# Delta-rule layers: the triangle's inverse made in full from 32x32 products, and one solution step in 32x32 tiles

## The reference

```python
def delta_rule(q, k, v, beta):
    def step(W, inp):
        qt, kt, vt, bt = inp
        wk = jnp.einsum('bhde,bhe->bhd', W, kt)
        v_new = bt * (vt - wk)
        W = W + jnp.einsum('bhd,bhe->bhde', v_new, kt)
        out = jnp.einsum('bhde,bhe->bhd', W, qt)
        return (W, out)
    ...
def fast_ff(x, ln_g, ln_b, slow_w, out_w):
    h = layer_norm(x, ln_g, ln_b)
    qkvb = jnp.einsum('sbi,oi->sbo', h, slow_w).reshape(slen, bsz, H, 3 * D + 1)
    q, k, v, beta = jnp.split(qkvb, [D, 2 * D, 3 * D], axis=-1)
    q = jax.nn.softmax(q, axis=-1)
    k = jax.nn.softmax(k, axis=-1)
    beta = jax.nn.sigmoid(beta)
    attn = delta_rule(q, k, v, beta)
```

## Time and profile before

| | us |
|---|---|
| median of 3 runs | 5387.88 |
| lowest, highest | 5385.71, 5416.66 |
| the profiled execution | 5345.09 |
| its span, first to last instruction | 5343.3 |

### The profile page before, as it was taken

How to read it: one execution, slowest core, us unless ns; L and a number is a source line. 1 busy time by engine, 2 the same in 40 slices (tenths; PEclk the granted TensorE clock), 3 DMA queues, 4 the chain that set the end, 5 groups by cost and what they waited for, 6 DMA issues and landing times. The chain is left out here.

```text
span 5343.3 us, 141254 instructions
## 1 busy us (share of the span) xinstructions
PE 4536.1 (85%) x57740; PEld 2868.5 (54%) x57741; DVE 2973.0 (56%) x5849; ACT 2153.1 (40%) x4123; POOL 853.9 (16%) x2139
## 2 busy tenths in 40 slices
PE   3678888888988988998777987799999999985995
PEld 1247777773437777774354654345454455443663
DVE  3445444453024444454577887488685885864343
ACT  1123232332123333231365566177575775741221
POOL 0000000000000000000454555011111111102112
PEclk7779888898988888798888988899999999996997
DMA  1000000000000000000100000000000000005223
GB/s 42 2 7 3 3 3 3 3 3 18 0 6 3 3 3 3 3 3 3 38 1 1 1 1 1 10 1 0 1 0 1 1 0 1 0 3 194 87 85 100
DMA packets 47557, 85.79 MB, mean 16 GB/s; under 512 B 7120, under 2 KB 38128, under 8 KB 46064
## 3 DMA queue, kind: packets, MB, share of 16 engines
q1 hardware_dynamic: 40944, 61.84, 3.4%
q0 software_dynamic: 6144, 16.79, 1.0%
HBM read 45.05 MB, written 33.55 MB: 15 GB/s over the span
## 5 line engine op out<-in xcount | busy, mean ns | idle before, releaser
L1769 PE MATMUL psum<-hm_ex,hm_mix 128*128 128x512 f32 x1024 | 510.9, 622 | 42.1 <-ACT hm_Aq L1849 38.1
L1835 ACT ACTIVATE hm_ex<-psum,hm_nm 128x1024 f32<-128x1024 f32 x256 | 285.5, 1115 | 300.6 <-DVE hm_nm L1893 300.6
L1769 PEld LDWEIGHTS psum<-hm_ex,hm_mix 128*128 128x128 f32 x1024 | 175.7, 191 | 353.1 <-issue 345.4
L1908 DVE COPY hm_A<-psum 128x1024 f32<-128x1024 f32 x256 | 312.9, 1222 | 51.5 <-PE psum L1778 47.8
L1903 DVE TENSOR_SCALAR_CACHE_REDUCE hm_plus<-hm_Aq,hm_cbcol,hm_sums 128x1024 f32<-128x1024 f32 x256 | 340.5, 1330 | 0.0
L1893 DVE TENSOR_REDUCE hm_nm<-psum 128x1 f32<-128x1024 f32 x256 | 311.1, 1215 | 14.5 <-PE psum L1757 14.5
L1778 PEld LDWEIGHTS psum<-K,hm_Aq 128*128 128x128 f32 x2048 | 236.7, 140 | 149.9 <-issue 145.2
L957 DVE TENSOR_TENSOR fw_M<-fw_M,psum 128x256 f32<-128x256 f32 x256 | 107.9, 421 | 344.9 <-PE psum L728 342.4
L1307 ACT ACTIVATE pt_signs<-pt_acts,pt_tb 128x1024 f32<-128x1024 f32 (+1 forms) x224 | 227.8, 1020 | 146.7 <-POOL pt_tb L1180 104.4
L1840 ACT ACTIVATE hm_junk<-hm_Aq 128x1024 f32<-128x1024 f32 x256 | 270.6, 1057 | 30.3
L1757 PE MATMUL psum<-hm_kt,hm_qd 64*32 64x512 f32 x4096 | 280.9, 607 | 0.0
(11 more groups left out here) (380 smaller groups left out, 9117.4 us busy)
## 6 DMA issues: line engine op xcount, KB each, us to landing
ex_rows_in<-ex_zero SPq DMA_DIRECT2D x2, 5120.0 KB, 24.8
ex_xs<-ex_rows_in SPq DMA_DIRECT2D x80, 128.0 KB, 2.0
ex_rows_out<-ex_ys SPq DMA_DIRECT2D x80, 128.0 KB, 1.7
ex_w<-in_ex_w SPq DMA_DIRECT2D x2, 4096.0 KB, 23.0
X<-in_x SPq DMA_DIRECT2D x2, 2048.0 KB, 12.5
out_y<-X SPq DMA_DIRECT2D x2, 2048.0 KB, 9.0
ff_w<-in_ff_w SPq DMA_DIRECT2D x2, 1024.0 KB, 5.9
pt_w_proc<-in_pt_proc SPq DMA_DIRECT2D x1, 2048.0 KB, 7.6
```

The costliest lines, as they stand in the source:

```text
L1769: mm = pe.matmul(bank[4 + c], mix[:, u, :], ex[:, u, 512 * c:512 * c + 512], start=True, stop=True)
L1835: act.activation(ex[:, u, :], flat2(psum[:, 2 * u:2 * u + 2, :]), ACT.Exp, bias=nm[:, u:u + 1], accum_out=rsum[:, u:u + 1]).then_inc(s_ex, 1)
L1908: dve.tensor_copy(A[:, :, :, QT_ * t:QT_ * t + QT_], flat2(psum[:, 6:8, :]).rearrange("p (m g n) -> p m g n", m=MT, g=HEADS)).then_inc(s_a ...
```

## The change

The inverse of the whole 32-token triangle is made for each group and head: with N the product of Z and the off-diagonal rest, the inverse is Z + (I - N + NN)(-NZ). It takes five more calls of `product`: the turn of `z3` by a unit matrix (`zn`, copied by ScalarE), the product `z3` and `loff` in both orientations (`nn`, copied with a factor of -1), then in the next body `nn` squared and `zn` by `nn`, and last `s1` by `nz`. VectorE makes `s1` in `series` and the inverse in `inverse`. `solve` is called once, as 8 heads x 4 groups = 32 matmuls with 32x32 weights and 64 columns. The copies `r0`, the eight copies of `spread` into `z3x` and `ntx`, and the two calls of `solution` are gone; `solved` copies from PSUM instead of adding, and stands ahead of `softmax` on VectorE. `turn` moves ahead of the products with `loff` on TensorE, and the copies of `tr` with it on ScalarE. Banks 2 and 5 are shared by halves. The diff, cut to its core:

```diff
-                def product(left, right):
+                def product(b, at, left, right, sig):
                     for n in range(HEADS):
+                        for c in range(4):
+                            mm = pe.matmul(bank[b][rows(c), at + DH * n:at + DH * n + DH], right[rows(c), n, :],
+                                           left(rows(c), n), start=True, stop=True)
+                    mm.then_inc(sig, 1)
...
+                def solve(a):
+                    for n in range(HEADS):
+                        hd = DH * (2 * (n % 4) + n // 4)
                         for b in range(4):
...
+                            mm = pe.matmul(bank[2][rows(b), 64 * n:64 * n + 64], inv[rows(b), n, :],
+                                           rhs[rows(b), a % 2, :, hd:hd + DH], start=True, stop=True)
+                    mm.then_inc(s_ap, 1)
...
                     if so:
-                        pe.wait_ge(s_zx, s + 1)
-                        solve(z3x, given, s_y)
                     if ch:
                         pe.wait_ge(s_trc, i + 1)
                         pe.sem_inc(s_go, 1)
                         gram(a, 0, s_ga)
+                    if so:
+                        pe.wait_ge(s_nn, s + 1)
+                        pe.wait_ge(s_zn, s + 1)
+                        pe.sem_inc(s_go, 1)
+                        product(5, 0, of(nn[:, 0]), nn[:, 1], s_nb)
+                        product(2, C, of(zn), nn[:, 0], s_nb)
...
-                    if so:
-                        pe.wait_ge(s_nt, s + 1)
-                        pe.wait_ge(s_r0, s + 1)
-                        solve(ntx, first, s_ap)
                     if rc:
                         pe.wait_ge(s_m, r * 5 + 2)
                         through_state(ra, 1)
+                    if so:
+                        pe.wait_ge(s_s1, s + 1)
+                        pe.wait_ge(s_nz, s + 1)
+                        pe.sem_inc(s_go, 1)
+                        product(2, 0, of(s1), nz, s_nc)
...
                         project(i + 1)
-                    if so:
-                        pe.wait_ge(s_rk, s * 2 + 1)
-                        solve(ntx, later, s_ap)
...
                     if rc:
                         pe.wait_ge(s_m, r * 5 + 3)
                         through_state(ra, 2)
+                    if so:
+                        pe.wait_ge(s_ix, s + 1)
+                        pe.sem_inc(s_go, 1)
+                        solve(sa)
...
-                    if so:
-                        pe.wait_ge(s_rk, s * 2 + 2)
-                        solve(ntx, later, s_ap)
...
+                    if nxt:
+                        turn(i + 1, (a + 1) % 4)
                     if ch:
                         pe.wait_ge(s_z, i * 2 + 2)
                         pe.wait_ge(s_lo, i + 1)
                         pe.sem_inc(s_go, 1)
-                        product(z3, loff)
-                    if nxt:
-                        turn(i + 1, (a + 1) % 4)
+                        product(2, 0, one, z3, s_zt)
+                        product(5, 0, of(z3), loff, s_na)
+                        product(5, C, of(loff), z3, s_na)
...
-                def solution(s, it):
-                    dve.wait_ge(s_ap, s * 3 + it + 1)
-                    dve.tensor_tensor(rk[:, :, :, :].rearrange("p n y e -> p (n y e)"), bank[2],
-                                      r0[:, :, :, :].rearrange("p n y e -> p (n y e)"), ALU.add).then_inc(s_rk, 1)
+                def series(s):
+
+                    dve.wait_ge(s_nb, s * 2 + 1)
+                    own.done(dve.tensor_tensor(s1[:, :, :], result(5), nn[:, 0], ALU.add))
+                    dve.tensor_tensor(s1[:, :, :], s1[:, :, :], small(2, HEADS), ALU.add).then_inc(s_s1, 1)
+
+                def inverse(s):
+                    dve.wait_ge(s_nc, s + 1)
+                    if since(s, 1):
+                        dve.wait_ge(s_ap, s)
+                    dve.tensor_tensor(inv[:, :, :], result(2), z3[:, :, :], ALU.add).then_inc(s_ix, 1)
```

More of the change, by code:

```diff
@@ L601, in fast_weight_stage @@
         compact = lambda n: sb(n, [P, HEADS, DH])
[L602 to L605, removed]
+        l8, l8t, bg, loff, qm, z1, z2, tt, z3, l2, zn, nz, s1, inv = (
+            compact(n) for n in "l8 l8t bg loff qm z1 z2 tt z3 l2 zn nz s1 inv".split())
+        nn = sb("nn", [P, 2, HEADS, DH])
         pu = sb("pu", [P, 2, C]); pk = sb("pk", [P, C]); pkt = sb("pkt", [P, 2, C])
@@ L693, in gram @@
                     mm.then_inc(sig, 1)
-                def product(left, right):
+                def product(b, at, left, right, sig):
                     for n in range(HEADS):
-                        for b in range(4):
[L698 to L705, removed]
+                        for c in range(4):
+                            mm = pe.matmul(bank[b][rows(c), at + DH * n:at + DH * n + DH], right[rows(c), n, :],
+                                           left(rows(c), n), start=True, stop=True)
+                    mm.then_inc(sig, 1)
+                of = lambda m: lambda r, n: m[r, n, :]
+                one = lambda r, n: k.const("small")[r, 2 * DH:3 * DH]
+                def solve(a):
+                    for n in range(HEADS):
+                        hd = DH * (2 * (n % 4) + n // 4)
+                        for b in range(4):
+                            mm = pe.matmul(bank[2][rows(b), 64 * n:64 * n + 64], inv[rows(b), n, :],
+                                           rhs[rows(b), a % 2, :, hd:hd + DH], start=True, stop=True)
+                    mm.then_inc(s_ap, 1)
                 def turn_keys():
@@ L775, in body @@
                         pe.sem_inc(s_go, 1)
-                        product(l8, l8t)
+                        product(5, 0, of(l8), l8t, s_t)
                     if rc:
@@ L790, in body @@
                         pe.sem_inc(s_go, 1)
-                        product(z1, l2)
+                        product(5, 0, of(z1), l2, s_t)
                     if rc:
@@ L797, in body @@
                         pe.sem_inc(s_go, 1)
-                        product(z2, l2)
+                        product(5, 0, of(z2), l2, s_t)
                     if rc:
@@ L808, in body @@
                         pe.sem_inc(s_go, 1)
-                        product(tt, l2)
+                        product(5, 0, of(tt), l2, s_t)
                     if rc:
@@ L843, in body @@
                     if so:
[L844 to L847, removed]
+                        act.wait_ge(s_nb, s * 2 + 2)
+                        act.activation(flat(nz[:, :, :]), bank[2][:, C:2 * C], ACT.Copy).then_inc(s_nz, 1)
                     if ch:
-                        act.wait_ge(s_t, i * 5 + 1)
+                        act.wait_ge(s_t, i * 4 + 1)
                         act.activation(flat(l2[:, :, :]), bank[5][:, 0:C], ACT.Copy).then_inc(s_l2, 1)
+                    if ch:
                         act.wait_ge(s_qm, i + 1)
@@ L880, in body @@
                                        ACT.Copy).then_inc(s_trc, 1)
+                    if ch:
+                        act.wait_ge(s_zt, i + 1)
+                        act.activation(flat(zn[:, :, :]), bank[2][:, 0:C], ACT.Copy).then_inc(s_zn, 1)
+                        act.wait_ge(s_na, i * 2 + 2)
+                        act.activation(nn[:, :, :, :].rearrange("p y h j -> p (y h j)"), bank[5], ACT.Copy,
+                                       scale=-1.0).then_inc(s_nn, 1)
                     if rc:
@@ L886, in _ @@
                 k.load_table(act, ACT.Exp)
-                act.wait_ge(s_zero, 6)
+                act.wait_ge(s_zero, 4)
                 k.credit(act, s_fin, 1)
@@ L991, in body @@
                         state(r, 0)
+                    if so:
+                        series(s)
                     if ch:
                         lower(i)
-                    if so:
-                        solution(s, 0)
                     if rc:
                         corrected(r, ra, 1)
+                    if so:
+                        inverse(s)
                     if ch:
@@ L1003, in body @@
                         less_max(i + 1)
-                    if so:
-                        solution(s, 1)
                     if ch:
@@ L1013, in body @@
                         state(r, 2)
+                    if so:
+                        solved(s, sa)
                     if nxt:
                         softmax(i + 1, (a + 1) % 4)
-                    if so:
-                        solved(s, sa)
                     if ch:
-                        if since(i, 1):
-                            dve.wait_ge(s_y, i)
                         factor(i, 4, z3, z2)
```

33 lines of the change are left out of this document (10 added, 23 removed).

## The result

The changed kernel takes 5825.4 us (median of 4 runs, 5818.6 to 5828.7) against 5396.8 us before (5385.7 to 5416.7): 1.079 times as long, 95% interval 1.075 to 1.083. It is 429 us slower; forecast were 5710 us in a range of 5500 to 5900.

A forecast was written before the change was run, and what follows sets the result against it. TensorE's instruction stream bounds the tile: 6.5 blocks at 3.9 us plus 4.9, 31.9 with half the tiles at half clock, plus 0.9 for jumps: 32.8 against 27.5. Times 60, +320 us on 5387.9 gives 5710; range 5500 to 5900.

The forecast's parts named there:

- The count of instructions: TensorE's stream per tile: 944 pairs of weight load and matmul plus some 29 waits, 1917 instructions, 7.5 blocks instead of 5.0.
- The time of a block: Fetching 256 TensorE instructions takes 3.9 us, mean of 3.5, 5.0, 3.5 and 3.6; ends of 3.5 and 5.0 kept.
- the 8 to 12 that I gave as a sign: Idle TensorE before loads in the middle of products, at places waiting for no data: 8 to 12 us a tile.
- The tile at the full clock: One loop tile: 6.5 blocks at 3.9 us plus 4.9 us for the block holding the projection, 30.3 us.
- The clock: TensorE's clock in the loops: half the tiles at each level, 31.9 us a tile; granted clock near 0.75.
- half clock throughout: Rival: all loop tiles at half clock, +420 us, 5810 us; 21% together with a fetch at the upper end.
- The waits costed at nothing: TensorE's waits for `lower` (1.2 us) and `turn` (2 us) would show, but vanish if TensorE is starved of instructions.
- The jump: The loop's jump back idles TensorE 3.6 us in four tiles, adding 0.9 us a tile, as before the change.
- The array's gain: Array time of a tile at the full clock: -7.7 + 3.6 + 1.0, net -3.1 us, 24.1 becomes 21.0.
- The new solution step: The 32x32 solution step with 64 columns, in no row, taken as 1.0 us of the array.
- fetching hides: Rival: instruction fetch costs no time in the loops, -1.3 to -3.4 us a tile, about -150 us, 5240 us; 13%.

The follow-up runs named there:

- e8: The changed kernel with the hardware loop of the delta-rule stage written out, no jump back: 5718 us, 1.058.
- e7: The kernel before with five unread 32x32 products more in every tile (944 pairs, as in the changed kernel), each set beside slow work: 5837 us, 1.081.
- e6: The kernel before with the hardware loop of the delta-rule stage written out, no jump back: 5304 us, 0.982.
- e2: The kernel before with 8 unread matmuls of 128x128 by 256 columns more in every tile, 32 instructions: 5456 us, 1.012.
- e5: The changed kernel with 8 unread matmuls of 128x128 by 256 columns more in every tile, as in e2: 5927 us, 1.097.

## Why the prediction was right

**The count of instructions: right.** 1917 a tile were forecast and 1915 are there, 190 packets in 24 tiles (7.9; without jumps, in e8, 178, which is 7.4).

**The time of a block: right, and right for the right reason.** 3.9 us were taken from four distances; the median in the changed kernel is 4.0 and the quickest tiles give 3.8 to 4.0. The rows hold seven distances, with 5.0 and 3.5 of the earlier trace rows and 4.5 us to the last packet of the earlier trace rows; their mean is 4.1, so the choice of four did little. The starts were not 3.5 to 5 us apart throughout, as I had written: 96 of 159 distances are, and most others are longer. The stops are 6.2 us a tile and 0.8 more at the jumps, less than the 8 to 12 that I gave as a sign.

**The tile at the full clock: right as far as it can be seen.** 30.3 was the sum; no tile of the changed loops ran at the full clock. Tiles of e7 with 7.5 blocks at that clock take 28.3 to 30.3, with 24.4 us of matmuls.

**The clock: wrong.** Forecast were half of the tiles at each level and about 0.75; the changed loops have 0.63, most of a tile at 1.2 GHz. That is the rival "half clock throughout", which gave 5810 us, and the measurement is 5825. My argument against it, that the array's work would fill the gaps at half clock, did not hold: the gaps stayed. With three quarters of the time at half, which is a granted clock of 0.63, the sum's own terms give 30.3 + 0.74 x 3.3 + 0.9 = 33.6 us a tile, and 34.4 and 33.5 were measured.

**The waits costed at nothing: half wrong, and their price is open.** I had `lower` and `turn` swallowed by the stops. `product(l8)` still waits 0.8 us a tile (19.5 / 24), and `turn` 0.9 us (13.3 and 7.8). A likely reason, argued and not tested: with one block fetched ahead, a wait that makes one block long is not got back in the next. But the sum without them gives 32.7 us for a tile without a jump at the clock that was granted, and these tiles average 32.7. So if the waits cost 1.7 us, other terms of the sum were too large by as much; luck may have its part in the total.

**The jump: too low.** 0.9 us a tile had been added on both sides; in fact it is 4.1 us of gap in the changed kernel, and a jump costs about 10 us with it and without the change (e6, e8), 2 us for each of the 24 tiles around the five jumps of a layer. As it is on both sides, the forecast difference hardly suffered.

**The array's gain was real and did not show.** The five products and the one solution step do cost less of the array than four full steps did: weight loads are busy 442 us in 24 tiles, at a lower clock, for 462 before. The new solution step, in no row before, loads for 0.93 us where 1.0 was taken. The rival "fetching hides" fails on the stops in the middle of products.

Against the forecast of +320 us (5.3 us for each of 60 tiles) the layers cost +437 (7.0 for each of 62). The tile of the changed kernel is 33.9 us where 32.8 were forecast, 0.8 of it by the clock alone, and that of before 27.0 where I had 27.5. So the cause and the time of a block were forecast, and the term that was mis-sized is the clock.

## What to carry to other kernels

Count the instructions of TensorE as a second budget beside its time: here 256 weight loads, matmuls and waits cost about 3.9 us or more however little they do, so a 32x32 float32 product of 128 instructions is 0.7 us of array and 2 us of stream. Replacing one large matmul by many small ones can pay only while the stretch around it holds more than 4 us of array work for each 256 instructions. Where a burst of small matmuls stops in its middle with nothing to wait for, put slow work beside it, share weights to save instructions, and write out a loop whose jump is followed by such a stop.

## What the runs showed that I had not expected

A jump back costs about 10 us of a layer, more than twice its visible gap. Added array work can be free: 3.4 us a tile in e2 cost nothing over 24 tiles of layer 1, where the granted clock went from 0.84 to 0.95. In e5 the clock rose as well (0.63 to 0.76), and the stops for instructions stayed at 149 us, so a faster clock doesn't shorten them; it shortens the matmuls between them.
